# A graph layer with experts on Trainium2: a wait ahead of each row gather, so that two are outstanding at most

## The chip, the cores and the metric

The kernel runs on one core of one Trainium2 chip. The metric is the time of one execution on the device in microseconds, taken without a profiler; several executions give a median. The engines are TensorE (matrix products), VectorE, ScalarE, GpSimd and SyncE; each has its own queue of instructions and they meet only at semaphores. DMAs are started by an engine and carried by 16 DMA engines, which all queues share.

## What is computed

The reference, cut to what matters (12500 nodes, 256 features, 212500 edges, 64 experts, two for each node):

```python
ones = jnp.ones((src.shape[0],), feats.dtype)
deg_out = jnp.clip(jax.ops.segment_sum(ones, src, num_segments=n), 1.0)
deg_in = jnp.clip(jax.ops.segment_sum(ones, dst, num_segments=n), 1.0)
h = feats * jax.lax.rsqrt(deg_out)[:, None]
m = jax.ops.segment_sum(h[src], dst, num_segments=n) * jax.lax.rsqrt(deg_in)[:, None]
gc = m @ W_gc + b_gc
x = gc + (feats @ W_res + b_res)
core = _moe_ff(x, Wg, bg, w1, b1, w2, b2)      # top-2 gates, gelu(h @ w1 + b1) @ w2 + b2
y = x + core
return (y - mean) * jax.lax.rsqrt(var + BN_EPS) * gamma + beta
# and around it: layernorm(x + layer(x))
```

The part that matters here is `h[src]` summed by `dst`: for each of the 212500 edges, sorted by destination, one row of 256 floats is fetched from a table of 12500 rows.

## The kernel before

The program has four stages. In the first (`columns_and_degrees`) edge lists become columns, the degrees are counted, and the scaled table `h_table` is written to device memory. The second (`aggregate`) gathers and sums, makes x1 and chooses the experts. The third (`experts`) runs the 64 experts, the fourth (`norms`) normalises.

The second stage goes over 98 tiles of 128 destination nodes. The edges are cut into 1661 chunks of 128; a tile has PER = 17 of them. For each chunk, 128 rows of 1 KB have to be in the slot `c % RING` of a ring of 38 slots (`got`, a view of `work`). Then TensorE multiplies a one-hot matrix, made by VectorE, with the 128 rows and adds the product to the tile's bank of PSUM (L1820). Every fourth chunk it raises `summed`.

The rows come in three ways. The first 27 chunks (READY) are fetched in the first stage. Of 105 chunks, about one for each tile, the first stage fetches the rows from x ahead of time, with GpSimd, and SyncE stores them in `x_ahead` (L690 and L638); in the second stage SyncE loads them from there with plain DMAs, and ScalarE scales them. All other 1529 chunks are fetched in the second stage by GpSimd, with one indirect DMA each, the loop in question:

- `fetched` is the list of these chunks, `fetch_of[c]` the number of a fetch in it.
- ahead of every fourth chunk GpSimd waits for `summed`, with FLIGHT = 24, so that fetches never run more than 24 chunks ahead of TensorE.
- each fetch raises by 16 one of 24 semaphores, `gathered[fetch_of[c] % FLIGHT]`, when it has landed. TensorE waits for it ahead of the chunk's product. Until now GpSimd itself doesn't wait for any landing there.

The order of everything in this stage is written out by hand, each engine's program tile by tile. On TensorE steps of former tiles stand between the chunks: after the chunk with k = 3 `product` (L1722, waits for ScalarE's copy `turned`), k = 13 `ranks`, k = 15 `turn_in` (the turns L1709 and L1711, which raise `m_turned`), k = 16 `list_places`. ScalarE copies the turned tile (L1380) when `m_turned` is reached. SyncE loads x, stores x + beta, loads the sums' start values `m_base` into `acc` (SET = 7 tiles at a time), clears `picked` (a fourteenth of it for each set), stores x1 rows, and loads from `x_ahead`.

In the first stage VectorE (L760, L762), ScalarE (L867) and TensorE (L931, L935) count degrees in a loop, while GpSimd fetches the rows for `x_ahead`. There six slots are in use in turn, and from the seventh on every fetch waits for the store that had the slot before.

Of the kernel before, what the change touches and what calls it, by code (L numbers as in the profile page):

```python
# [54 lines left out]
def gnn_layer(nc, x, src, dst, W_gc, b_gc, W_res, b_res, Wg, bg, w1, b1, w2, b2, gamma, beta, out):  # L55
# [37 lines left out]
    with ExitStack() as ctx:  # L93
# [204 lines left out]
        with ExitStack() as stage:  # L298
            def tmp(name, shape, dt):
                return stage.enter_context(nc.sbuf_tensor(name, shape, dt))  # L300

            W1, W2 = HELD * KD * H, HELD * KH * D
            assert W1 + W2 + HELD * D <= (RING + 1) * (D + 1)
            w1s = work[:, 0:W1].rearrange("p (u k h) -> p u k h", u=HELD, k=KD)
            w2s = work[:, W1:W1 + W2].rearrange("p (u k d) -> p u k d", u=HELD, k=KH)
            b2s = work[:, W1 + W2:W1 + W2 + HELD * D].rearrange("p (u d) -> p u d", u=HELD)
            table = tmp("table", [P, 4, (X + HELD) * (CAP // P)], F32)
            base_of = tmp("base_of", [1, X + 2 + HELD], I32)
            b1_cols = tmp("b1_cols", [P, KH, X], F32)
            w_in = [ctx.enter_context(nc.semaphore(f"w_in{u}")) for u in range(HELD)]  # L310

            def load_weights(eng, e, u):

                eng.dma_start(w1s[:, u, :, :], w1[bass.ds(e, 1), :, :].rearrange("a (k p) h -> p (a k) h", p=P)).then_inc(w_in[u], 16)
                eng.dma_start(w2s[:, u, :, :], w2[bass.ds(e, 1), :, :].rearrange("a (k p) d -> p (a k) d", p=P)).then_inc(w_in[u], 16)
                eng.dma_start(b2s[:, u, :], b2[bass.ds(e, 1), :].broadcast_to([P, D])).then_inc(w_in[u], 16)

            with nc.cleanup_on_exit():
                aggregate(nc, x, W_res, b_gc, b_res, W_gc, Wg, bg, b1, beta, h_table, x1_rows, x_beta, picked, m_base, flag_i, base_out, zeros_out, y_total, acc3, work, ident, ones,
                          iota_f, place_lo, src_cols, rel_cols, where, valid, f_edge, f_lanes, x_ahead, extra_f_in, early_set, table, base_of, b1_cols, load_weights, ps,  # L320
                          N=N, D=D, X=X, H=H, KD=KD, KH=KH, AW=AW, CH=CH, PER=PER, EARLY=EARLY, LATE=LATE, NT=NT, LAST=LAST)
            experts(nc, x1_rows, picked, w1s, w2s, b2s, w_in, load_weights, ident, ones, table, base_of, b1_cols, y_total, acc3, ps, N=N, D=D, X=X, H=H, KD=KD, KH=KH,
                    ROW=ROW, PLACES=NPAD * TOP_K)
# [776 lines left out]
def aggregate(nc, x, W_res, b_gc, b_res, W_gc, Wg, bg, b1, beta, h_table, x1_rows, x_beta, picked, m_base, flag_i, base_out, zeros_out, y_total, acc3, work, ident, ones, iota_f,  # L1100
# [3 lines left out]
    with ExitStack() as part:  # L1104
# [3 lines left out]
        def sem2(name):  # L1108
            return nc.alloc_semaphore(name)

        MW = D + 1
        FLIGHT = 24
        BANKS = 3
        HALF = (PER + 1) // 2
        HALVES = ((0, HALF), (HALF, PER))
# [16 lines left out]
        assert FIRST_AHEAD - 2 > RANKS_LAG  # L1132
        assert EARLY + LATE + 2 + FLIGHT <= RING and LAST_OF < FIRST_OF and CAP % P == 0 and X * SLOTS <= BANK
        got_flat = work[:, 0:(RING + 1) * MW]
# [10 lines left out]
        fetch_of = {c: i for i, c in enumerate(fetched)}  # L1145
# [67 lines left out]
        lanes_set = sem2("lanes_set")  # L1213
        gathered = [sem2(f"gathered{k}") for k in range(FLIGHT)]
        hot_set = sem2("agg_hot_set")
# [52 lines left out]
        def groups(n):  # L1268
            return (n + GROUP - 1) // GROUP
# [13 lines left out]
        with nc.Block() as block:  # L1283
            @block.sync
            def _(sp):
# [21 lines left out]
                def load_ahead(n):  # L1307
                    sp.wait_ge(summed, groups(ahead[n] + 1 - FLIGHT))
                    sp.dma_start(got[:, ahead[n] % RING, 0:D], x_ahead[n * P:(n + 1) * P, :]).then_inc(rows_ahead_in[n % 2], 16)

                def load_extra(n):
                    sp.wait_ge(summed, groups(extra_chunks[n] + 1 - FLIGHT))
                    sp.dma_start(got[:, extra_chunks[n] % RING, 0:D],
                                 x_ahead[(AHEAD + n) * P:(AHEAD + n + 1) * P, :]).then_inc(rows_extra_in, 16)
# [105 lines left out]
            @block.gpsimd  # L1420
            def _(pool):
                for c in range(READY, CH):
                    if c + GROUP > RING and c % GROUP == 0:
                        pool.wait_ge(summed, groups(c + GROUP - FLIGHT))
                    if c in ahead or c in extra_chunks:
                        continue
                    pool.indirect_dma_start(out=got[:, c % RING, 0:D], out_offset=None, in_=h_table[:, :],  # L1427
                                            in_offset=bass.IndirectOffsetOnAxis(ap=src_cols[:, c:c + 1], axis=0)).then_inc(gathered[fetch_of[c] % FLIGHT], 16)

            @block.vector  # L1430
            def _(dve):
# [26 lines left out]
                def evict(t):  # L1458
                    dve.wait_ge(tile_done, t + 1)
                    if t % SET == 0:  # L1460
                        dve.wait_ge(base_in[t // SET % 2], 16 * (t // SET // 2 + 1))
                    nc.vector.tensor_tensor(acc3[:, t, 0:MW], acc3[:, t, 0:MW], ps[:, t % BANKS, 0:MW], ALU.add).then_inc(evicted, 1)

# [211 lines left out]
            def _(pe):  # L1675
                def begin(t):
                    if t >= BANKS:
                        pe.wait_ge(evicted, t - BANKS + 1)
                    nc.tensor.matmul(ps[:, t % BANKS, 0:MW], none[:, :], none_w[:, 0:MW], start=True, stop=False)

                def end(t):
                    nc.tensor.matmul(ps[:, t % BANKS, 0:MW], none[:, :], none_w[:, 0:MW], start=False, stop=True).then_inc(tile_done, 1)

                def extra(t, place):
                    pe.wait_ge(hot_x_set, t)
                    nc.tensor.matmul(ps[:, t % BANKS, 0:MW], hot_x[:, t % 2, :], got_flat[:, bass.ds(place, MW)],
                                     start=False, stop=False).then_inc(extra_summed, 1)
# [110 lines left out]
                for t in range(NT):  # L1798
                    of = chunks(t)
                    _, w = nc.values_load_multi_w_load_instructions(  # L1800
                        where[0:1, t:t + 1], engines=[EngineType.PE], min_val=0, max_val=(RING + 1 << PER) - 1,
                        skip_runtime_bounds_check_because="a bit for each chunk, then a place in the ring")
# [589 lines left out]
```

## Time and profile before

| | us |
|---|---|
| median of 3 executions without a profile | 3363.47 |
| lowest and highest of them | 3356.97, 3364.64 |
| span of the profiled execution | 3782.8 |
| TensorE busy in it | 2867.3 (76%) |
| VectorE busy | 2006.0 (53%) |
| GpSimd busy | 2109.8 (56%) |
| ScalarE busy | 1197.5 (32%) |

The profile is one execution, recorded by the hardware; its span is from the first to the last instruction. It lasts 419 us longer than the median without a profile. Engines in the rows are PE (TensorE's products), PEld (its weight loads), DVE (VectorE), ACT (ScalarE), POOL (GpSimd), SPq (SyncE's queue). L1427 is line 1427 of the kernel. "Idle before" is time in which the engine stood still just before an instruction, and "<-" names who ended it: an engine's instruction, a DMA, "issue" for nothing that the profile shows, "remote" for an update of a semaphore without a recorded instruction behind it. Ends of products are modelled.

### The profile page before, as it was taken

To read this page: it belongs to the slowest core of one execution; us is meant where nothing else is said; L and a number is where in the kernel's file an instruction comes from. 1 tells how busy PE (TensorE), PEld (TensorE's weight loads), DVE (VectorE), ACT (ScalarE), POOL (GpSimd) and SP (SyncE) were. 2 spreads that over 40 slices of the span, in tenths; PEclk is the share of its full clock that TensorE was granted. 3 is DMA by queue.
4 is the path that set the end of the run, shared out by engine and by line. 5 is a ranking of instruction groups with operands and counts; after the bars stand their busy time and mean duration, and the time that the engine had idled before them with its cause. 6 is when DMAs were issued, how large, how long until landed. Compare 5 with 4: busy or idle time off the path is not lost. (4 is left out here: it accounts for less than half of the span.)

```text
span 3782.8 us, 61265 instructions
## 1 busy us (share of the span) xinstructions
PE 2867.3 (76%) x15295; PEld 2136.6 (56%) x15296; DVE 2006.0 (53%) x7025; ACT 1197.5 (32%) x2890; POOL 2109.8 (56%) x2156
## 2 busy tenths in 40 slices
PE   3245778787777877777777777778699999999950
PEld 3234445555545545555554555555588989888840
DVE  5369444444544444454444444444555555555598
ACT  3368112222222222222212222212244444444428
POOL 5722666666666666666666666665355555555500
PEclk7557888998998888989889888989899999999985
DMA  7622534444444434444344444434444454444387
GB/s 245 188 68 89 175 114 137 117 141 119 142 144 119 136 117 137 148 117 138 118 138 121 146 137 119 137 109 126 142 139 138 149 161 136 148 136 151 99 312 233
DMA packets 309520, 537.64 MB, mean 142 GB/s; under 512 B 47197, under 2 KB 220381, under 8 KB 307698
## 3 DMA queue, kind: packets, MB, share of 16 engines
q0 software_dynamic: 102160, 273.85, 24.8%
q1 hardware_dynamic: 206766, 259.99, 20.8%
q8 instruction: 80, 1.31, 0.1%
q10 hardware_dynamic: 436, 1.85, 0.1%
q14 instruction: 78, 0.64, 0.1%
HBM read 418.03 MB, written 121.75 MB: 143 GB/s over the span
## 5 line engine op out<-in xcount | busy, mean ns | idle before, releaser
L1427 POOL DMA_INDIRECT work<-h_table,src_cols x1529 | 1456.6, 953 | 785.1 <-issue 419.1
L1820 PE MATMUL ps<-work 128*128 128x257 f32 x3322 | 1056.8, 400 | 36.9 <-issue 35.0
L1820 PEld LDWEIGHTS ps<-work 128*128 128x128 f32 x3322 | 621.1, 198 | 290.7 <-issue 114.4
L1691 PE MATMUL ps<-none_w,none 128*128 128x512 bf16 x1369 | 534.2, 390 | 14.1 <-issue 13.6
L2091 PEld LDWEIGHTS ps<-xst,work 128*128 128x128 f32 x3648 | 443.4, 192 | 28.9 <-issue 17.9
L2091 PE MATMUL ps<-xst,work 128*128 128x128 f32 x3648 | 447.4, 276 | 11.6 <-issue 11.6
L1966 POOL DMA_INDIRECT picked<-ys,places x228 | 249.2, 1093 | 357.5 <-DVE ys L2036 334.8
L2098 PE MATMUL ps<-work,hid 128*128 128x256 f32 x1824 | 436.6, 382 | 0.3
L1722 PE MATMUL ps<-w_conv,turned 128*128 128x320 f32 x392 | 173.7, 579 | 268.5 <-ACT turned L1380 181.1
L1947 ACT ACTIVATE hid<-ps,b_cols 128x128 f32<-128x128 f32 x912 | 304.1, 367 | 186.2 <-PE ps L2091 119.2
L2098 PEld LDWEIGHTS ps<-work,hid 128*128 128x128 f32 x1824 | 329.0, 190 | 46.3 <-ACT hid L1947 10.5
L1540 DVE TENSOR_SCALAR lane_hi<-ps,rt_parts 128x128 bf16<-128x128 f32 x196 | 67.7, 345 | 454.1 <-remote 446.7
L1959 POOL DMA_INDIRECT ring<-x_rows,rows_at x230 | 224.8, 978 | 131.3 <-issue 73.4
L1722 PEld LDWEIGHTS ps<-w_conv,turned 128*128 128x128 f32 x392 | 87.4, 242 | 325.4 <-ACT turned L1380 193.9
L1447 DVE TENSOR_TENSOR work<-rel_cols,ps 128x1152 f32<-128x1152 f32 x196 | 250.5, 1279 | 16.0 <-remote 8.6
L1380 ACT COPY turned<-ps 128x512 f32<-128x512 f32 x98 | 57.4, 586 | 618.7 <-remote 587.2
L1374 ACT COPY acc<-ps 128x256 f32<-128x256 f32 x98 | 36.5, 372 | 603.0 <-remote 372.6
L867 ACT ACTIVATE stairs<-iota_f,work 128x128 bf16<-128x128 f32 x624 | 184.1, 387 | 129.4 <-remote 111.6
L1494 DVE TENSOR_TENSOR logits<-ps,gate_bias 128x64 f32<-128x64 f32 x98 | 21.9, 224 | 352.4 <-issue 177.0
L2051 DVE TENSOR_TENSOR ysum<-ps,work 128x256 f32<-128x256 f32 x228 | 96.9, 425 | 204.7 <-PE ps L2098 169.1
L931 PE MATMUL ps<-work 128*128 128x98 bf16 x1040 | 83.7, 241 | 150.8 <-issue 117.5
L1942 ACT COPY xs<-ring 128x256 f32 (+1 forms) x230 | 93.1, 405 | 327.0 <-POOLq L1986 187.2
(309 smaller groups left out, 4244.3 us busy)
## 6 DMA issues: line engine op xcount, KB each, us to landing
work<-in_L_gnn_w_dram SPq DMA_DIRECT2D x128, 512.0 KB
picked<-work SPq DMA_DIRECT2D x14, 1792.0 KB
work<-h_table,src_cols POOLq DMA_INDIRECT x1529
pk<-picked SPq DMA_DIRECT2D x13, 1792.0 KB
x_ahead<-work SPq DMA_DIRECT2D x105, 128.0 KB
work<-x_ahead SPq DMA_DIRECT2D x105, 128.0 KB
acc<-m_base SPq DMA_DIRECT2D x14, 903.0 KB
x_beta<-xr_x SPq DMA_DIRECT2D x98, 128.0 KB
```

Of the source, the lines that this page charges most:

```text
L867: mm = nc.scalar.activation(stairs[:, k, n, :], iota_f[:, :], ACT.Sign, scale=-1.0, bias=lo_half[:, bass.ds(g * PIECES + 2 * WHOLE + n, 1)])
L1427: pool.indirect_dma_start(out=got[:, c % RING, 0:D], out_offset=None, in_=h_table[:, :], in_offset=bass.IndirectOffsetOnAxis(ap=src_cols[: ...
L1447: nc.vector.tensor_tensor(hot[:, (2 * t + h) % HOTS, 0:b - a, :], rel_cols[:, a:b].unsqueeze(2).broadcast_to([P, b - a, P]), lanes.unsquee ...
L1691: nc.tensor.matmul(ps[:, 7, :], none[:, :], none_w[:, :], start=False, stop=False)
L1722: nc.tensor.matmul(ps[:, 5, 0:DX], turned[:, k, :], w_conv[:, k, :], start=(k == 0), stop=False)
L1820: mm = nc.tensor.matmul(ps_flat[:, bank(t, k, w[0])], hot[:, (2 * t + (k >= HALF)) % HOTS, k % HALF if k >= HALF else k, :], got[:, c % RI ...
L1947: nc.scalar.activation(hid[:, h, :], ps[:, h, 0:SUP], ACT.Gelu, bias=b1_cols[:, h, bass.ds(e, 1)]).then_inc(h_set, 1)
L1959: pool.indirect_dma_start(out=ring[:, u, :], out_offset=None, in_=x1_rows[:, :], in_offset=bass.IndirectOffsetOnAxis(ap=rows_at[:, u:u + 1 ...
L1966: pool.indirect_dma_start(out=picked[:, :], out_offset=bass.IndirectOffsetOnAxis(ap=places[:, u:u + 1], axis=0), in_=ys[:, u, :], in_offse ...
L2051: nc.vector.tensor_tensor(ysum[:, :], ps[:, 4, 0:D], b2s[:, u, :], ALU.add).then_inc(ysum_set, 1)
L2091: mm = nc.tensor.matmul(ps[:, h, 0:SUP], w1s[:, u, k, h * P:(h + 1) * P], xst[:, k, :], start=(k == 0), stop=(k == KD - 1))
L2098: mm = nc.tensor.matmul(ps[:, 4, 0:D], hid[:, h, :], w2s[:, u, h, :], start=(h == 0), stop=(h == KH - 1))
```

## The change

Ahead of each fetch of the second stage GpSimd waits until the fetch two places before it in the list has landed. So no more than two fetches are outstanding at a time. The wait for `summed` stays. The first two fetches have none of the new waits.

```diff
         FLIGHT = 24
+        IN_FLIGHT = 2
         BANKS = 3
...
                     if c in ahead or c in extra_chunks:
                         continue
+                    before = fetch_of[c] - IN_FLIGHT
+                    if before >= 0:
+                        pool.wait_ge(gathered[before % FLIGHT], 16 * (before // FLIGHT + 1))
                     pool.indirect_dma_start(out=got[:, c % RING, 0:D], out_offset=None, in_=h_table[:, :],
                                             in_offset=bass.IndirectOffsetOnAxis(ap=src_cols[:, c:c + 1], axis=0)).then_inc(gathered[fetch_of[c] % FLIGHT], 16)
```

No instruction changes its place. GpSimd's rows at the start of the stage, before (several semaphores of this stage appear in such rows under the name of a semaphore of an earlier block that had the same number, such as `any_gathered4`):

```order
L1427 DMA work<-h_table,src_cols 128x256 x9
L1427 DMA work<-h_table,src_cols 128x256 [waits summed]
L1427 DMA work<-h_table,src_cols 128x256 x3
L1427 DMA work<-h_table,src_cols 128x256 [waits summed]
L1427 DMA work<-h_table,src_cols 128x256 x3
```

And the same place with the change:

```order
L1431 DMA work<-h_table,src_cols 128x256 x2
L1431 DMA work<-h_table,src_cols 128x256 [waits any_gathered4]
L1431 DMA work<-h_table,src_cols 128x256 [waits any_gathered5]
L1431 DMA work<-h_table,src_cols 128x256 [waits any_gathered6]
L1431 DMA work<-h_table,src_cols 128x256 [waits any_gathered7]
L1431 DMA work<-h_table,src_cols 128x256 [waits any_gathered8]
L1431 DMA work<-h_table,src_cols 128x256 [waits any_gathered9]
L1431 DMA work<-h_table,src_cols 128x256 [waits any_gathered10]
L1431 DMA work<-h_table,src_cols 128x256 [waits any_gathered11,summed]
L1431 DMA work<-h_table,src_cols 128x256 [waits any_gathered12]
```

Each fetch from the third on now waits for one landing more; every fourth still waits for `summed` too.

## Rows read from the trace of the kernel before

**Rows 1.** The profile page, its first line: the span and the instructions.

```profile
span 3782.8 us, 61265 instructions
```

**Rows 2.** Busy time in stretches: us; PE, PEld, DVE, ACT, POOL; clock; DMA share; GB/s.

```profile
175.00:217.00 42.00, 0.62 (x8) 0.40 (x5) 0.00 (x0) 0.00 (x0) 31.73 (x34) 0.50 0.71 205
...
395.00:2645.00 2250.00, 1755.80 (x7307) 1153.34 (x7306) 1070.13 (x4220) 470.47 (x780) 1456.12 (x1529) 0.90 0.43 130
2700.00:3595.00 895.00, 865.69 (x5860) 795.50 (x5858) 495.90 (x1875) 391.68 (x1128) 468.22 (x452) 1.00 0.45 141
```

**Rows 3.** GpSimd's waits, 395 to 2660: us in total, times, longest us.

```profile
POOL work L1427 <- issue: 419.1, 1355, 2.9
POOL work L1427 <- remote: 240.3, 111, 3.1
POOL work L1427 <- PE ps L1820: 119.7, 62, 4.9
```

**Rows 4.** GpSimd in order of time: start us, us, what, [idle before <-releaser].

```profile
1017.77 0.95 POOL L1427 DMA_INDIRECT work<-h_table,src_cols  x1 [0.30 <-issue]
1021.36 0.94 POOL L1427 DMA_INDIRECT work<-h_table,src_cols  x1 [2.64 <-remote]
```

**Rows 5.** Other engines in order of time, and TensorE's waits from 60 to 352.

```profile
1008.81 0.27 PE L1711 MATMUL ps<-ident,xr_x 128*128 128x128 f32 x1
...
1019.60 0.59 ACT L1380 COPY turned<-ps 128x512 f32<-128x512 f32 x1 [11.14 <-remote]
...
217.17 0.98 DVE L760 TENSOR_TENSOR work<-hi_b,values 128x1568 bf16<-128x1568 bf16 x1 [43.10 <-remote]
...
PE ps L931 <- issue: 115.8, 13, 43.3
```

**Rows 6.** A fetch after a pause, and busy time around it in steps of 0.2 us.

```profile
1003.97 0.95 POOL L1427 DMA_INDIRECT work<-h_table,src_cols  x1 [1.80 <-remote]
...
1005.40:1005.60 0.20, 0.00 (x0) 0.00 (x0) 0.20 (x2) 0.00 (x0) 0.20 (x1) 1.00 0.00 0
1005.60:1005.80 0.20, 0.00 (x0) 0.00 (x0) 0.20 (x2) 0.00 (x0) 0.20 (x1) 1.00 0.81 184
...
1006.20:1006.40 0.20, 0.20 (x3) 0.01 (x1) 0.20 (x1) 0.00 (x0) 0.00 (x0) 1.00 0.08 21
```

**Rows 7.** Fetches for `x_ahead` to 167.5, stores to 170.55, by line; each one's last.

```profile
L690 POOL DMA_INDIRECT work<-in_x_dram,src_cols x67: 945/949/1600, 68.5 to 167.5; - x67
...
  issue: 20.3, 66
...
L638 SPq DMA_DIRECT2D x_ahead<-work x67: 319/320/353, 74.5 to 170.5; - x67
...
167.47 0.94 POOL L690 DMA_INDIRECT work<-in_x_dram,src_cols  x1 [0.30 <-issue]
...
170.52 0.32 SPq L638 DMA_DIRECT2D x_ahead<-work  x1
```

**Rows 8.** The expert stage's first fetches, GpSimd in order of time.

```profile
2681.00 0.95 POOL L1959 DMA_INDIRECT ring<-x_rows,rows_at  x1 [50.82 <-DVE rows_at L2012]
2682.25 0.95 POOL L1959 DMA_INDIRECT ring<-x_rows,rows_at  x1 [0.31 <-issue]
2686.41 0.95 POOL L1959 DMA_INDIRECT ring<-x_rows,rows_at  x1 [3.22 <-DMA ring<-x_rows,rows_at]
2688.54 0.94 POOL L1959 DMA_INDIRECT ring<-x_rows,rows_at  x1 [1.18 <-DMA ring<-x_rows,rows_at]
```

**Rows 9.** DMA issues of the page, KB each; and a crowded stretch.

```profile
picked<-work SPq DMA_DIRECT2D x14, 1792.0 KB
...
acc<-m_base SPq DMA_DIRECT2D x14, 903.0 KB
...
x_rows<-acc SPq DMA_DIRECT2D x13, 903.0 KB
...
1268.00:1280.00 12.00, 11.75 (x53) 7.88 (x51) 6.16 (x30) 3.66 (x6) 6.64 (x7) 1.00 0.99 329
```

## The prediction

> **What bounds the kernel now.** I read the views in this order: the span, busy time by stage, GpSimd's row and waits in the gather stage, then short timelines and fine windows for the life of one fetch.
>
> The profiled execution has a span of 3782.8 us [rows 1], 419 us above the median of 3363.5 us of the runs without a profile. So the profile shows something that the timed runs don't have, and the sum needs to know where it sits. The stage with the gathers lasts from about 395 to 2645 us [rows 2]: 2250 us, 59% of the span. GpSimd starts 1529 fetches in it, with 1456.1 us busy, 0.95 us each.
>
> GpSimd is idle 419.1 us in 1355 short gaps of some 0.30 us and 360.0 us in 173 longer ones (240.3 in 111 and 119.7 in 62) [rows 3]. The longer ones are stops: after the fetch at 1017.77 the next one starts at 1021.36, behind 2.64 us [rows 4]. Back to back a fetch costs 0.95 + 0.30 = 1.25 us. In a stop it waits for `summed`: the ring is full, TensorE is behind. So in the profiled execution the gathers are not the bound, they stand a whole ring ahead.
>
> But TensorE is behind for an odd reason. The turns of x start at 1008.81, and ScalarE's copy of what they made starts only at 1019.60, after 11.14 us of idle time ended by something that the profile doesn't name; in between GpSimd goes on fetching [rows 4, 5]. The same silence is in the stage before: VectorE waits 43.10 us until 217.17, has 0.00 us of work from 175 to 217, and TensorE's L931 waits 115.8 us in 13 such idle times, all while GpSimd fetches rows for `x_ahead` [rows 2, 5]. The expert stage can't hide 419 us: TensorE is busy 865.7 of 895.0 us there [rows 2].
>
> Now without these silences. The gather stage would go at GpSimd's own pace: 1456.1 + 419.1 + 173 x 0.30 = 1927 us, and some 16 us from the last fetch at about 2629 to 2645, so 1943 us: 307 less than 2250. The early stage would lose 115.8. Together 423 us, against the 419 that are missing. I take this as the likeliest account: in the timed runs GpSimd's fetch rate bounds the gather stage, at 1.25 us a fetch, and **whatever slows a fetch is paid 1529 times**. That is an inference from two sums that agree within 4 us, not a view of an unprofiled run.
>
> **The change.** Nothing is removed and nothing moves. All fetches but the first two, 1527 of 1529, get one wait. Satisfied waits are cheap: the fetches for `x_ahead`, of which all but the first six carry a wait on a landing, have 66 gaps with 20.3 us together, 0.31 each, as the gaps without waits [rows 7]. So the wait costs only its length. Queued behind it on GpSimd are only the further fetches. TensorE waits for those by chunk; VectorE, ScalarE and SyncE follow TensorE.
>
> With two outstanding, fetch c starts when c-2 has landed and GpSimd has woken. So two fetches take L, the time from the start of one to the release of whoever waits for it, and the pitch is L/2, if that is above 1.25. The break-even is L = 2.5 us.
>
> L has bounds from three rows. **Below:** after a pause a fetch starts at 1003.97; the 16 DMA engines move nothing until 1005.60 and its bytes end between 1006.20 and 1006.40 [rows 6]. That is 2.43 us at most, before the semaphore is told; with the usual 0.30 us gap before an instruction, L = 2.73. **The nearest row:** the 67th fetch for `x_ahead` starts at 167.47 (128 rows of 1 KB, as here), and SyncE's 67th store, which waits for just that landing, at 170.52 [rows 7]. That is L = 3.05, with the semaphore and a wake-up inside. **Above:** the expert stage begins with this very pattern, two fetches and a third that waits for the first. They start at 2681.00, 2682.25 and 2686.41, the fourth at 2688.54: L = 5.41 and 6.29 us, with weights loading beside them [rows 8]. As quiet values I keep 2.73 and 3.05 + 0.30 = 3.35 as ends, and take 3.05, because it is the same transfer with a real waiter. The 5.4 to 6.3 I use for crowded stretches.
>
> Quiet sum: 1529 x 3.05 / 2 = 2332 us.
>
> Crowded stretches: every seven tiles there is a clearing of `picked` (1792 KB) with a store of x1 rows (903 KB) and, apart from it, a load of `acc` (903 KB) [rows 9]. From 1268 to 1280 the DMA share is 0.99 for the first two [rows 9]. With a third of that for the load, 16 us by 14 are 224 us. At a pitch of 2.9 (the mean of 5.41 and 6.29, halved) instead of 1.53, 224 x (1/1.53 - 1/2.9) = 69 fetches are missing, 106 us at 1.53. The ring's lead doesn't cover this, since fetching is the bound and never regains a lead.
>
> After: 2332 + 106 + 16 = 2454 us for the stage, against 1943: **+511 us**. On the median that is 3363.5 + 511 = 3875 us, 15% slower. In the profile I expect 3782.8 - 2250 + 2454 = 3987 us, if the early silences stay.
>
> With the ends: L = 2.73 gives 2087 + 118 + 16 = 2221, +278, 3642 us; L = 3.35 gives 2561 + 95 + 16 = 2672, +729, 4092 us.
>
> Other edits: none. SyncE's loads into `x_ahead` slots wait for `summed` and come later with TensorE, hidden as before.
>
> One rule speaks for a smaller loss. The trace shows 2.43 us to the last bytes and 3.05 us to a waiter [rows 6, 7]. The Trainium skill, "DMA: Bandwidth & Descriptors", section "Anatomy of one DMA — SWDGE (gpsimd) path", fits such a DMA as 2.0 us plus bytes over 436e3, so an estimate of 2.3 us for 128 KB. With 0.30 us for the gap its L would be 2.6, the pitch 1.30, and the result near 3545 us; the row with a real waiter speaks against it.
>
> **The rivals.**
> *The loop closes in time.* Two fetches are outstanding already: at a pitch of 1.25 and 2.43 us to the last byte there are 1.9 in flight on average. If release and wake-up took under 0.08 us, L would be below 2.5 and the wait would be free in quiet stretches. Only the crowded ones cost: 224 x (1/1.25 - 1/2.9) x 1.25 = 127 us, so 3491 us. For it: the 2.43 us of rows 6. Against it: the 3.05 us of rows 7. Chance 0.07.
> *The stage is paced by TensorE's tile loop also without a profile.* Then the silences are real and the 419 us lie elsewhere. The stage lasts 2250 us before and 2454 after: +204, 3568 us. For it: the stops of rows 3 are there. Against it: no stage has 419 us to give. Chance 0.08.
> *The other side: pauses free the other engines.* The silences end when GpSimd pauses: the copy at 1019.60 comes just after the fetch of 1017.77 to 1018.72 [rows 4, 5]. If they occur in timed runs too, a GpSimd that waits after each fetch gives its pause 1529 times, and the silences go. The stage is then bound by the fetches alone and is faster if the pitch with its crowded stretches is below 2250 / 1529 = 1.47 us. At L = 2.73 it takes 2221 us, 29 less: 3335 us. It needs both the real silences and the lowest L. Chance 0.04. By the Trainium skill, "SBUF — State Buffer", section "Who interferes with whom", VectorE in some modes and GpSimd lock each other out of a shared port, which would fit VectorE's idle time; here TensorE's result is late as well, which that rule doesn't say.
>
> **How the numbers follow.** The forecast has 0.81, with its own ends at 3642 and 4092; most of it below 4060. The predicted time is its 3875 us. The range goes from 3600, which leaves out the rivals (0.19) and little else, to 4060. A measurement of this kernel can tell about 0.3% from no change. Faster by more: 0.04. Within 0.3%: 0.02, for a wait that is free in crowded stretches too. Slower: 0.94.
>
> **What the profile after would show.** Right: GpSimd's idle time before the fetches has releaser DMA or "remote" nearly each time, the pitch is 1.5 to 1.65 us, starts two apart differ by some 3.05 us, the stage is about 2450 us long, and waits for `summed` are gone. TensorE waits at L1820's line for landings instead of for turned tiles, and the 10 us silences are shorter or gone, so the profile lies nearer to the timed runs than the 419 us of before. Wrong: fetches still 1.25 us apart (the first rival), or a profile whose stage grows by 200 us and a median that does the same (the second). If L is right and the stage grows otherwise, the account of the 419 us is what failed.

## The result and the profile after

The kernel with the change takes 4085.1 us in the median (4083.7 to 4087.1), the kernel before 3363.1 us: a ratio of 1.216, 95% interval 1.214 to 1.217. It is 722 us slower. The forecast was 3875 us, 512 us slower, with a range of 3600 to 4060: the direction and the stage were right, the size fell out of the range.

From the profile's page after: the span, then the two costliest lines (busy us, mean ns of one | idle before, by releaser).

```profile
span 4081.6 us, 61532 instructions
...
L1431 POOL DMA_INDIRECT work<-h_table,src_cols x1529 | 1450.2, 948 | 1214.0 <-DMA work<-h_table,src_cols 1056.2
L1824 PE MATMUL ps<-work 128*128 128x257 f32 x3322 | 1177.6, 438 | 724.9 <-DMA work<-h_table,src_cols 700.1
```

GpSimd's idle time before its fetches was 419.1 + 240.3 + 119.7 = 779.1 us, with no landing among the releasers [rows 3]; now 1056.2 of 1214.0 us are ended by landings of the fetches themselves. TensorE waits for them too, 700.1 us. The page has no wait for `summed` worth a line any more. The answer for the fetches' line after (min/median/max ns of one, first and last start; idle time by releaser; landing measured from the start):

```profile
L1431 POOL DMA_INDIRECT work<-h_table,src_cols x1529: 940/944/1202, 292.6 to 2934.0; - x192
...
  DMA work<-h_table,src_cols: 1056.2, 1217
...
DMA to landing us min/median/max: 2.6/2.8/8.4
```

1528 steps from 292.6 to 2934.0 are a pitch (mean time from fetch to fetch) of 1.729 us; the landing takes 2.8 us in the median. The forecast had named a pitch of 1.5 to 1.65 us and a stage of about 2450 us as signs of being right; the stage is 2646 us (the columns are those of [rows 2]):

```profile
292.00:2938.00 2646.00, 1917.69 (x7157) 1093.39 (x7297) 1073.37 (x4222) 469.83 (x779) 1450.21 (x1529) 0.93 0.37 111
```

Fetch by fetch, GpSimd after (start us, us, what):

```profile
1000.68 0.94 POOL L1431 DMA_INDIRECT work<-h_table,src_cols  x1 [1.17 <-DMA work<-h_table,src_cols]
1001.92 0.94 POOL L1431 DMA_INDIRECT work<-h_table,src_cols  x1 [0.30 <-issue]
1004.16 0.94 POOL L1431 DMA_INDIRECT work<-h_table,src_cols  x1 [1.29 <-DMA work<-h_table,src_cols]
1005.41 0.94 POOL L1431 DMA_INDIRECT work<-h_table,src_cols  x1 [0.30 <-issue]
1007.13 0.94 POOL L1431 DMA_INDIRECT work<-h_table,src_cols  x1 [0.78 <-DMA work<-h_table,src_cols]
```

These are the chunks 458 to 462. From 1004.16 to 1007.13, two fetches apart, it is 2.97 us: the loop of the forecast (3.05). But from 1000.68 to 1004.16 it is 3.48 us, in as quiet a moment. The fetch at 1004.16 is chunk 460, a multiple of four: it waits for `summed` as well.

### The profile page after: what moved, and what is told of

The parts are those of the page before. It is cut to its first block and busy times, and to the rows that moved or that the text cites. A ratio compares the mean times of both kernels' runs of the same rounds, so it can differ in the third digit from the quotient of the medians.

```text
span 4081.6 us, 61532 instructions
## 1 busy us (share of the span) xinstructions
PE 3022.0 (74%) x15155; PEld 2067.1 (51%) x15296; DVE 2012.2 (49%) x7025; ACT 1208.3 (30%) x2890; POOL 2124.3 (52%) x2156
## 5 line engine op out<-in xcount | busy, mean ns | idle before, releaser
L1431 POOL DMA_INDIRECT work<-h_table,src_cols x1529 | 1450.2, 948 | 1214.0 <-DMA work<-h_table,src_cols 1056.2
L1824 PE MATMUL ps<-work 128*128 128x257 f32 x3322 | 1177.6, 438 | 724.9 <-DMA work<-h_table,src_cols 700.1
L1824 PEld LDWEIGHTS ps<-work 128*128 128x128 f32 x3322 | 561.4, 200 | 1299.1 <-issue 1040.7
L1695 PE MATMUL ps<-none_w,none 128*128 128x512 bf16 x1244 | 489.9, 394 | 0.0
L1951 ACT ACTIVATE hid<-ps,b_cols 128x128 f32<-128x128 f32 x912 | 316.8, 367 | 162.1 <-PE ps L2095 115.9
L1371 ACT ACTIVATE acc<-acc,f_in 128x256 f32<-128x256 f32 x98 | 49.8, 509 | 493.6 <-DVE f_in L1482 493.6
L2022 DVE COPY xst<-ps 128x256 f32<-128x256 f32 x229 | 97.2, 425 | 128.6 <-PE ps L2088 122.3
L1695 PEld LDWEIGHTS ps<-none_w,none 128*128 128x128 bf16 x1369 | 138.6, 101 | 37.1 <-issue 0.2
```

What stands on the lines that cost most here:

```text
L1695: nc.tensor.matmul(ps[:, 7, :], none[:, :], none_w[:, :], start=False, stop=False)
L1824: mm = nc.tensor.matmul(ps_flat[:, bank(t, k, w[0])], hot[:, (2 * t + (k >= HALF)) % HOTS, k % HALF if k >= HALF else k, :], got[:, c % RI ...
L1951: nc.scalar.activation(hid[:, h, :], ps[:, h, 0:SUP], ACT.Gelu, bias=b1_cols[:, h, bass.ds(e, 1)]).then_inc(h_set, 1)
L2022: nc.vector.tensor_copy(xst[:, :, :], ps[:, 6, 0:KD * SUP].rearrange("p (k n) -> p k n", k=KD)).then_inc(xst_set, 1)
```

## The experiments

**The kernel before, profiled again.** No edit.

> The kernel before, profiled once more. The forecast took the 419 us by which the first profile was longer than the timed runs for silences of TensorE, VectorE and ScalarE during GpSimd's fetches that timed runs don't have. If that is right, a second profile may come without them: span near 3361 us, the gather stage about 1929 us long (1529 fetches 1.25 us apart, some 13 us from the last to the stage's end), no stops of GpSimd at summed to speak of, TensorE waiting for landings. Rival (the silences belong to the kernel and its time): a span near 3780 again, stage near 2250.

Measured: 3358.0 us, span 3355.9. Its page, the answer for the fetches, and two stretches (us; PE, PEld, DVE, ACT, POOL; clock; DMA share; GB/s):

```profile
span 3355.9 us, 61125 instructions
...
L1427 POOL DMA_INDIRECT work<-h_table,src_cols x1529: 942/946/1205, 293.4 to 2213.8; - x192
...
  issue: 456.3, 1498
...
175.00:217.00 42.00, 28.73 (x390) 21.24 (x389) 40.94 (x49) 42.00 (x145) 34.56 (x24) 0.89 0.51 150
...
293.00:2218.00 1925.00, 1693.38 (x7158) 1092.35 (x7298) 1072.54 (x4222) 470.89 (x779) 1451.85 (x1529) 0.96 0.50 152
```

Where [rows 2] have 0.00 us of VectorE and ScalarE from 175 to 217, they are now busy for 40.94 and 42.00 us. The gather stage lasts 1925 us instead of 2250, with 1.257 us from fetch to fetch and 1498 of 1529 gaps without a wait that counts. ScalarE's copy of the turned tile no longer waits 11 us:

```profile
1008.71 0.58 ACT L1380 COPY turned<-ps 128x512 f32<-128x512 f32 x1 [2.24 <-PE ps L1711]
```

So the silences belonged to that one profiled execution. The forecast had put 307 us of them in the gather stage and 116 us ahead of it; by this profile it is 325 us (2250 less 1925) and 101 us (the first fetch of the stage starts at 293.4 instead of 394.5). Without them the kernel is bound by GpSimd's fetches in this stage, as the forecast had worked out (1943 us of stage). What causes such silences in a profile stays open.

**The two waits in the other order.**

```diff
-                    if c + GROUP > RING and c % GROUP == 0:
-                        pool.wait_ge(summed, groups(c + GROUP - FLIGHT))
+                    must = c + GROUP > RING and c % GROUP == 0
                     if c in ahead or c in extra_chunks:
+                        if must:
+                            pool.wait_ge(summed, groups(c + GROUP - FLIGHT))
                         continue
                     before = fetch_of[c] - IN_FLIGHT
                     if before >= 0:
                         pool.wait_ge(gathered[before % FLIGHT], 16 * (before // FLIGHT + 1))
+                    if must:
+                        pool.wait_ge(summed, groups(c + GROUP - FLIGHT))
```

> With the change, in the profile, a fetch with one wait starts 0.61 us after the last byte of the fetch it waits for, one that waits for summed as well (407 of 1529) 1.09 us after it. Here the two waits stand in the other order: the landing first, summed last. Theory A (whichever of two waits ends late, the wait that doesn't ride on the DMA's own instruction costs 0.48 us once it is over): the order decides which one that is; if the landing wait is now the one on the DMA's own instruction, the extra goes and the time falls by 100 to 190 us, to 3895 to 3985. If it was so already, the time stays. Theory B (any fetch with two waits is late by 0.48 us): 4085 in either order.

Measured: 3953.8 us, ratio to before 1.177 (1.175 to 1.179): 131 us less than the change. The answer for the fetches, and GpSimd in order of time, chunks 493 to 496:

```profile
L1434 POOL DMA_INDIRECT work<-h_table,src_cols x1529: 940/944/1203, 292.4 to 2809.0; - x192
...
1017.38 0.94 POOL L1434 DMA_INDIRECT work<-h_table,src_cols  x1 [0.58 <-DMA work<-h_table,src_cols]
1018.89 0.94 POOL L1434 DMA_INDIRECT work<-h_table,src_cols  x1 [0.57 <-DMA work<-h_table,src_cols]
1020.36 0.95 POOL L1434 DMA_INDIRECT work<-h_table,src_cols  x1 [0.52 <-DMA work<-h_table,src_cols]
1021.85 0.95 POOL L1434 DMA_INDIRECT work<-h_table,src_cols  x1 [0.54 <-DMA work<-h_table,src_cols]
```

Chunk 496, at 1021.85, has both waits and starts 2.96 us after chunk 494. The 0.5 us are gone. They stay for 30 of the 407: where the multiple of four is itself not fetched here (its rows come from `x_ahead`), the wait for `summed` still comes first. So the order decides, theory A. Theory B falls. The pitch is 1.647 us (292.4 to 2809.0).

The trace also shows which of the two waits stands on an instruction of its own. With the change GpSimd's queue has 407 instructions at the fetch's lines that do nothing but wait; in the reversed order 377 stand at L1433, and the 30 others at L1431:

```profile
L1430 POOLq EVENT_SEMAPHORE x407: 17/17/17, 311.8 to 2933.3; - x136
...
L1433 POOLq EVENT_SEMAPHORE x377: 17/17/17, 311.4 to 2807.1; - x189
```

It is the wait written last. In the change, the one ahead of chunk 460's fetch names the semaphore of chunk 458's fetch in its record and comes at 1003.44, when that fetch has landed (1003.42); the fetch itself, at 1004.16, carries `summed`. In the reversed order it names `summed` and is over at 1020.15, long before the landing at 1021.59 that chunk 496 waits for; the fetch itself carries the landing. From the landing to the start of the fetch that waited for it, by the records of both traces, it is 0.26 us in the median where the fetch carries that wait, and 0.74 us where the instruction ahead of it does, also for the 30. The difference is 0.48 us. (The last byte comes 0.35 us ahead of the landing, which gives the 0.61 and 1.09 us of the expectation.) So the wait that ends last should be written first.

**The wait for `summed` at every 16th chunk.**

```diff
+        EVERY = 16
...
-                    if c + GROUP > RING and c % GROUP == 0:
-                        pool.wait_ge(summed, groups(c + GROUP - FLIGHT))
+                    if c + EVERY > RING and c % EVERY == 0:
+                        pool.wait_ge(summed, groups(c + EVERY - FLIGHT))
```

> With the change, but the wait for summed only at every 16th chunk (for a product 8 chunks before, which TensorE has long done at this pace), so about 104 fetches with two waits instead of 407. If the second wait costs 0.48 us and the slower of the two alternating chains of fetches sets the pace, 380 x 0.48 = 183 us are in the time now and three quarters of it go: about 3948 us. If the two chains share it, half: about 4016. If the second wait costs nothing and the missing time lies in latency under load: 4085.

Measured: 3978.0 us (ratio 1.185, 1.183 to 1.187), 107 us less than the change, between the two expectations of 137 and 69. By this run all 407 second waits cost 107 x 4/3 = 143 us; the run before took the delay from 377 of them, and 131 x 407/377 = 142 us agrees. The two chains of fetches neither wait fully for the slower one nor share fully.

**The second wait on every fetch.**

```diff
-                    if c + GROUP > RING and c % GROUP == 0:
-                        pool.wait_ge(summed, groups(c + GROUP - FLIGHT))
+                    if c + GROUP > RING:
+                        pool.wait_ge(summed, groups(c // GROUP * GROUP + GROUP - FLIGHT))
```

> With the change and its order of waits (summed first, landing last), but with the wait for summed at every chunk, so that all 1527 fetches have two waits instead of 407. Theory (a fetch with both waits starts 1.09 us after the last byte it waits for instead of 0.61): the quiet pitch is (2.43 + 1.09) / 2 = 1.76 us instead of 1.52, with the 0.13 us that the version with reversed order lies above its quiet pitch 1.89, against its 1.647: 1529 x 0.243 = 371 us more than its 3954, so about 4325 us. Rival (what reversing the order gave back came from something else, such as the place of the wait for summed): 4085.

Measured: 4298.2 us (ratio 1.280, 1.278 to 1.283), 344 us above the reversed order, where 371 were expected and the rival had 4085. GpSimd's fetches in order of time:

```profile
1002.51 0.94 POOL L1431 DMA_INDIRECT work<-h_table,src_cols  x1 [0.91 <-DMA work<-h_table,src_cols]
1004.22 0.94 POOL L1431 DMA_INDIRECT work<-h_table,src_cols  x1 [0.76 <-DMA work<-h_table,src_cols]
1005.98 0.94 POOL L1431 DMA_INDIRECT work<-h_table,src_cols  x1 [0.82 <-DMA work<-h_table,src_cols]
1007.74 0.94 POOL L1431 DMA_INDIRECT work<-h_table,src_cols  x1 [0.81 <-DMA work<-h_table,src_cols]
```

Two apart are now 3.47 and 3.52 us, whichever chunk it is. The cost of about 0.5 us per fetch with two waits is shown from both sides.

**Eight outstanding.**

```diff
-        IN_FLIGHT = 2
+        IN_FLIGHT = 8
```

> Eight outstanding instead of two, all waits still there. The slowest landing seen under load took 8 us from its start, and 8 fetches take GpSimd 10 us at 1.25, so hardly a wait is ever unfulfilled. If waits cost only what they wait: the time of the kernel before, 3357 to 3365 us. If 1527 fulfilled waits, 407 of them on an instruction of their own, cost 0.05 us each: 3434.

Measured: 3358.3 us, ratio 1.0002 (0.9992 to 1.0012). From the answer for the fetches:

```profile
  DMA work<-h_table,src_cols: 7.6, 25
```

1521 waits, 25 of them for something, 7.6 us: waits that are fulfilled cost nothing that can be measured, with a second wait or without. The second wait's 0.5 us are due only where the fetch has to wait.

**Three outstanding,** in the change's order and in the reversed one.

```diff
-        IN_FLIGHT = 2
+        IN_FLIGHT = 3
```

> Three outstanding instead of two. Two apart plus one: a loop of 3.03 to 3.51 us by three is 1.01 to 1.17 us, below GpSimd's own 1.25, so quiet stretches cost nothing. In the crowded ones (some 224 us, loop 5.4 to 6.3 us, pitch 1.95) 224 x (1/1.25 - 1/1.95) = 64 fetches or 80 us are lost: 3440 us. If a wait cost something by itself, whether it is satisfied or not, it would be paid here by all 1527 fetches: at 0.1 us each 3590.

> Three outstanding, with the landing wait first and summed last. With the change's order three outstanding gave 3508 us: 64 of its fetches waited with two waits, at 0.48 us more each, about 31 us if each of these delays reaches the end. So about 3477 us. If with three outstanding the loop's length no longer matters, 3508.

Measured: 3508.1 us (ratio 1.045, 1.043 to 1.046) and 3486.5 us (1.038, 1.036 to 1.040). Both show the same: the quiet fetches are free, since a third of the loop is 1.0 us; the slow landings are not. In the change's order:

```profile
  issue: 435.6, 1355
  DMA work<-h_table,src_cols: 176.6, 149
```

149 fetches waited for a landing, 1.2 us each. I had expected 80 us of loss and it is 151: the first sign, beside the change itself, that the term for slow landings was too small. The reversed order gave back 22 us, of 31 expected; its loss, 127 us against the kernel before measured with it, is still well above 80.

**One outstanding,** in the reversed order.

```diff
-        IN_FLIGHT = 2
+        IN_FLIGHT = 1
```

> One outstanding, landing wait first. The pitch should be one whole loop: 2.43 us from a fetch's start to its last byte and 0.61 to the next start are 3.04 us, plus 0.2 us of slow landings on average (the mean landing with two outstanding is 2.60 us, not 2.43), 3.24 us. Then 1529 x (3.24 - 1.647) = 2436 us more than the 3954 of two outstanding: about 6390 us. If part of the 2.43 us comes from the other fetch in flight, it is less: at 2.2 us to the last byte about 6040.

Measured: 6227.5 us in one execution, of 6390 expected. GpSimd in order of time, and the landings:

```profile
2000.39 0.94 POOL L1434 DMA_INDIRECT work<-h_table,src_cols  x1 [2.12 <-DMA work<-h_table,src_cols]
2003.35 0.94 POOL L1434 DMA_INDIRECT work<-h_table,src_cols  x1 [2.02 <-DMA work<-h_table,src_cols]
2006.36 0.95 POOL L1434 DMA_INDIRECT work<-h_table,src_cols  x1 [2.06 <-DMA work<-h_table,src_cols]
...
DMA to landing us min/median/max: 2.6/2.8/8.2
```

The loop is 2.96 and 3.01 us long in quiet moments with a single fetch in flight as well: it is latency, not a share of bandwidth. On average it is 3.134 us. With two outstanding the pitch was 1.647, which is 0.08 us more than half of that. Of this 0.05 us is that landings take longer on average with two outstanding (2.94 us against 2.84 by the records, halved). The other 0.03 us would fit a slow landing in one chain of fetches that delays the other chain too; no run tests that by itself.

**Without 13 of the 14 clearings of `picked`,** on the version in reversed order and on the kernel before.

```diff
-                        sp.wait_ge(zeros_out, 16 * SETS)
+                        sp.wait_ge(zeros_out, 16)
...
-                    if slot % SET == 2 and slot < NT:
+                    if slot == NT - SET + 2:
                         clear_picked(slot // SET)
```

> Two outstanding, landing wait first (the version of 3954 us), and 13 of the 14 clearings of picked left out (each 1792 KB of zeros written while the gathers run; the last stays). The pitch of 1.647 us lies 0.13 above the quiet 1.515, 202 us in all, where the forecast had 106 for stretches in which such transfers crowd the DMA engines. The clearings are half of those bytes. Theory (the forecast's mechanism, mis-sized): 80 to 110 us go, 3845 to 3875. Rival (the slow landings don't come from these transfers but are spread over all fetches): 3954 less 20 at most.

> The kernel before, without 13 of the 14 clearings of picked. Its gathers are 1.257 us apart, where GpSimd alone needs 1.253, so slow landings cost it nothing while the ring is ahead: 3350 to 3360 us. If it is faster by more than 20 us, crowded DMA engines cost the kernel before too, and the comparison with the version above has to be corrected by that.

Measured: 3912.1 us, 42 us less than with them; and 3357.8 us, ratio 1.0002 (0.9993 to 1.0012), no change. The kernel before pays nothing for the clearings, the limited one does, but the clearings carry only half of what I had given them. The answer for the fetches in the limited version without clearings:

```profile
  DMA work<-h_table,src_cols: 946.8, 1373
...
DMA to landing us min/median/max: 2.6/2.8/7.4
```

Where the rest comes from I worked out from the DMA packets of the trace with them (reversed order, two outstanding). Of 1529 fetches 1089 had almost no packets of other queues beside their own and took 2.41 us in the median from their start to their last byte. The other 440 took longer, together 257 us above that. 56 of these, where others took most of the engines' time, account for 155 us; the other 102 us are small delays of 0.1 to 0.4 us, beside loads and stores of 128 KB of which each tile has three. No run took these small ones away, so their share is read from the trace and not shown by an experiment. What such lateness costs can be checked on the clearings: without them the mean time from a fetch's start to its last byte fell from 2.590 to 2.533 us, 87 us over 1529 fetches, and the kernel by 42 us. With two outstanding, lateness counts about half.

## Why the prediction was wrong in size

**What bounds the kernel: right.** The stage before lasts 1925 us in a profile without silences, forecast 1943, and the change costs it 1528 x (1.729 - 1.257) = 721 us, all of the 722 us of the median. The first profile's stops at `summed` [rows 3, 4] are not there in the profile whose span agrees with the timed runs (13.1 us in 30 waits are left). Reading them as slack would have led to the second rival and to about 3570 us.

**The quiet loop: right.** Forecast 3.05 us, from the store that waited for a landing [rows 7]. Measured 2.96 to 3.01 us. The first rival, a loop that closes within 2.5 us, fell, and with it the estimate from the Trainium skill, "DMA: Bandwidth & Descriptors", section "Anatomy of one DMA — SWDGE (gpsimd) path": its 2.3 us for 128 KB stand against 2.8 us to landing in the median in every run here; the measurement decides.

**The step that failed: "Satisfied waits are cheap ... So the wait costs only its length."** This was inferred from fetches that carry one wait each. In the change 407 fetches carry two, the new one last. Where such a fetch has to wait, it starts about 0.5 us later than one with a single wait. Since the build puts the wait written last on an instruction of its own, it is the landing that such a fetch learns of late: 0.74 us after it, not 0.26. That is worth 131 us (377 of them, reversed order) to 143 us (all of them, from every 16th). The forecast says that every fetch gets one wait and that the wait for `summed` stays; what the two do together was not asked. That fulfilled waits are cheap is right by itself (eight outstanding); the landing waits here are not fulfilled ones.

**The term that was too small: crowded stretches, 106 us.** In the reversed order the pitch is 1.647 against the quiet (2.42 + 0.61) / 2 = 1.515: 202 us. The forecast took the large transfers of each set of tiles as the whole of it. For those it was not too small: the 56 fetches beside them are 155 us late, about 78 us of time at one half, and leaving out the clearings gave back 42 us, where the forecast's way of counting has about half of 106. What it put at nothing are the many small delays (102 us late, about 51 us of time) and a remainder of 202 - 78 - 51 = 73 us, which no run separates: it holds the 30 fetches whose second wait still counts, and what slow landings do to the other chain. A loop whose mean is what counts was priced by its quiet value.

Sum of the misses: 131 for the second waits, 96 for slow landings (202 - 106), less 15 for the quiet loop (1529 x (1.525 - 1.515)): 212 us, against 4085.1 - 3875 = 210. By stages, the stage after is 2646 - 2454 = 192 us longer than forecast, and the stage before 1943 - 1925 = 18 us shorter, also 210; the first sum leaves out small terms (the 18 us, a shorter tail after the last fetch) that nearly cancel.

**The other side** (pauses free the other engines) fell: the silences aren't in the timed runs, and TensorE waits 700 us for landings. The expected span of 3987 us in the profile, with early silences, was wrong in that the profile after has none: it lies 3.5 us from its median.

**The range** held the uncertainty of the quiet loop from 2.73 to 3.35 us, and the quiet loop was the term that I knew best. Nothing in it stood for a cost that no row showed, nor for the spread of the landings. The forecast's own upper sum, 4092 with L = 3.35, lies near the measured time only by luck: the quiet loop isn't 3.35. The range's upper end of 4060 was 25 us too low.

## What to carry to other kernels

A limit on outstanding transfers is free only while limit x issue pitch exceeds the whole loop, from issue to landing to the next issue, at its slow end and not at its median. Here the loop is 3.0 us, up to 8 us beside other transfers, and the pitch 1.25: two cost 722 us, three 151 (127 in the better order), eight nothing. Where a DMA of GpSimd has to have two waits, write the one that ends last first, or let it have one; other instructions were not tried. And when a profile's span is far from the timed runs, find the missing time before pricing anything: a second profile of the same kernel settles it.

## What the runs showed of the hardware

- A fetch of 128 rows of 1 KB by GpSimd lands 2.6 to 2.7 us after its start at the least and 2.8 us in the median, with one, two, three or eight outstanding alike; the longest landings were 7.4 to 8.9 us, beside other transfers.
- A DMA instruction of GpSimd with two waits, of which the one written last is unfulfilled, starts 0.74 us after the landing, one that carries the landing's wait itself 0.26 us after it (3.48 us against 2.97 two apart). The wait written last is a queue instruction of its own (407 of them in the trace). Fulfilled, the second wait costs nothing (ratio 1.0002).
- One profiled execution of the kernel before was 419 us longer than its timed runs, with TensorE, VectorE and ScalarE silent for up to 43 us while GpSimd fetched. None of the later profiles had this.
